# Feed-forward's last two slots begun in the next block, the differential token transposes behind the mask, and products of constants at two passages

## Time and profile before

| | |
|---|---|
| median of 3 runs | 1691.2 us (1690.83 to 1692.31) |
| the profiled execution | 1685.52 us |
| its span, first to last instruction | 1683.8 us |
| its mean granted TensorE clock | 0.984 of full |
| TensorE busy | 95% of the span |
| VectorE, ScalarE, GpSimd busy | 70%, 54%, 40% |
| block 1 ends, block 2 begins | about 395 us |
| block 2 ends, block 3 begins | about 1052 us |
| experts begin | 1599 us |

### The profile page before, as it was taken

The page is one execution under the profiler, slowest core; times in us unless marked ns, Lnnn a source line. Parts: engine busy times, 40 slices in busy tenths (PEclk is TensorE's granted clock), DMA queues, the critical chain, the costliest instruction groups (busy, mean ns, idle before and its releaser), DMA issues. The chain is left out here.

```text
span 1683.8 us, 51948 instructions
## 1 busy us (share of the span) xinstructions
PE 1605.1 (95%) x18158; PEld 1337.3 (79%) x18158; DVE 1183.5 (70%) x3386; ACT 909.4 (54%) x2619; POOL 677.9 (40%) x1070
## 2 busy tenths in 40 slices
PE   7999999998999999999999998899999999999595
PEld 6887788786777777777777776799999999999564
DVE  6889888676777776676777766366777777777654
ACT  5777777543454444454455444555555556565241
POOL 3666655312233333333333332234444444444345
PEclk9999999999999999999999999899999999999898
DMA  3214212121220001110000001121212212122231
GB/s 103 65 47 122 71 55 58 44 57 45 50 53 26 25 26 29 29 28 25 25 25 25 25 27 27 37 58 45 61 46 56 59 42 61 45 56 57 83 95 42
DMA packets 157655, 82.30 MB, mean 49 GB/s; under 512 B 17642, under 2 KB 153116, under 8 KB 157569
## 3 DMA queue, kind: packets, MB, share of 16 engines
q1 hardware_dynamic: 154800, 77.68, 17.3%
q0 software_dynamic: 2048, 3.15, 0.6%
q10 hardware_dynamic: 720, 0.33, 0.1%
HBM read 61.03 MB, written 21.27 MB: 49 GB/s over the span
## 5 line engine op out<-in xcount | busy, mean ns | idle before, releaser
L1445 PE MATMUL bank<-diff_xT,diff_w_score 128*128 128x128 f32 x2048 | 258.9, 280 | 0.8 <-ACT diff_xT L1557 0.8
L1445 PEld LDWEIGHTS bank<-diff_xT,diff_w_score 128*128 128x128 f32 x2048 | 241.5, 193 | 22.4 <-issue 20.2
L1564 ACT ACTIVATE diff_keys<-bank 128x512 f32<-128x512 f32 x256 | 152.4, 595 | 165.3 <-PE bank L1445 165.3
L1754 POOL TENSOR_TENSOR diff_prob<-diff_prob,diff_inv_sum 128x512 f32<-128x512 f32 x64 | 67.2, 1050 | 379.9 <-DVE diff_inv_sum L1657 379.9
L2233 POOL TENSOR_TENSOR lat_prob<-lat_prob,lat_inv_sum 128x512 f32<-128x512 f32 x128 | 133.6, 1044 | 211.0 <-DVE lat_inv_sum L2158 210.0
L2033 ACT ACTIVATE lat_prob<-bank,lat_neg_max 128x128 f32<-128x128 f32 x512 | 180.5, 372 | 1.0 <-DVE lat_neg_max L2178 1.0
L2044 ACT ACTIVATE lat_query<-bank 128x512 f32<-128x512 f32 x128 | 76.4, 597 | 176.6 <-PE bank L1928 176.6
L1958 PE MATMUL bank<-lat_catT,lat_query 128*128 128x128 f32 x1024 | 143.3, 283 | 3.9 <-ACT lat_query L2044 3.9
L1928 PE MATMUL bank<-lat_catT,lat_w_score 128*128 128x128 f32 x1024 | 140.5, 281 | 2.5 <-ACT lat_catT L2025 1.0
L1958 PEld LDWEIGHTS bank<-lat_catT,lat_query 128*128 128x128 f32 x1024 | 126.0, 194 | 16.0 <-issue 10.6
L1938 PE MATMUL bank<-lat_probT,lat_c_rep 32*128 32x256 f32 x2048 | 128.3, 387 | 3.1 <-DVE lat_z L2163 3.1
(11 more groups left out here) (272 smaller groups left out, 3663.6 us busy)
## 6 DMA issues: line engine op xcount, KB each, us to landing
lat_c_rep<-cat SPq DMA_DIRECT2D x128, 128.0 KB
stage<-low_y SPq DMA_DIRECT2D x64, 64.0 KB, 1.6
diff_x_rep<-stage SPq DMA_DIRECT2D x128, 32.0 KB, 1.8
lat_c_t<-cat SPq DMA_DIRECT2D x32, 128.0 KB, 2.2
exp_w<-in_L_ffn_w_dram SPq DMA_DIRECT2D x16, 256.0 KB, 3.1
expert_rows<-latw_zeros SPq DMA_DIRECT2D x4, 548.0 KB, 5.5
exp_rows<-expert_rows SPq DMA_DIRECT2D x8, 274.0 KB, 3.8
low_x_t<-in_x_dram SPq DMA_DIRECT2D x32, 64.0 KB, 1.9
```

The costliest lines, as they stand in the source:

```text
L1445: last = nc.tensor.matmul(ring[(k + d) % 2][:, j * P:(j + 1) * P], w_score[:, H1 * (k // 2) + HS * d + 4 * (k % 2) + j, :], xT[:, :], star ...
L1564: nc.scalar.activation(keys[:, k // 2, 4 * (k % 2):4 * (k % 2) + 4, :].rearrange("p h t -> p (h t)"), ring[(k + d) % 2][:, :], ACT.Copy).t ...
```

## The change

Three edits.

1. The feed-forward's slots 16 and 17 leave block 1 and become the first work of block 2 on TensorE, VectorE, GpSimd and SyncE (`drain`). The feed-forward's tiles, its weights `w_out` and its semaphores are kept over the passage for that. SyncE's wait for the stored groups comes behind its work for pair 0.
2. In block 2 the transpose of the next pair's tokens comes behind the scores and their mask instead of in front of them.
3. `keep_busy` makes products of the bf16 identity with itself repeated (128 x 512, a constant) into a PSUM bank that nobody reads: eight at the end of block 2, 22 between the latent attention and the experts.

```diff
+    def keep_busy(self, bank, count):
+        wide = self.identb[:, None, :].to_broadcast([P, 4, P])
+        for _ in range(count):
+            self.nc.tensor.matmul(bank[:, :].rearrange("p (n d) -> p n d", n=4), self.identb[:, :], wide, start=True, stop=True)
...
@@ FeedForward @@
-        for g in range(NG - 4, NG + 2):
+        for g in range(NG - 4, NG):
             written(g)
+
+    def drain(self, eng, slot):
+        for g in range(self.NG, self.NG + 2):
+            slot(g, g // 4, g % 4, lambda d: 0 <= g + d < self.NG)
...
-    def tensor(self, pe, between=None):
+    def tensor(self, pe, between=None, drain=False):
...
-        pe.wait_ge(self.low.qT_ready, NI)
-        self.slots(pe, slot, between)
+        if drain:
+            self.drain(pe, slot)
+        else:
+            pe.wait_ge(self.low.qT_ready, NI)
+            self.slots(pe, slot, between)
...
@@ differential_attention_phase, sync @@
-            for par in range(2):
-                sp.wait_ge(ffn_stored[par], 16 * (FeedForward.NG // 2))
-            pairs(sp, pair, lambda i: latent.sync(sp, i))
+            def feed_forward_stored(i):
+                if i == 0:
+                    for par in range(2):
+                        sp.wait_ge(ffn.stored[par], 16 * (ffn.NG // 2))
+
+            ffn.sync(sp, drain=True)
+            pairs(sp, pair, lambda i: (feed_forward_stored(i), latent.sync(sp, i)))
...
@@ differential_attention_phase, tensor @@
-                    if d == 1 and more(i):
-                        transpose_x(i + 1)
                     if have(i):
                         if d == 0:
                             pe.wait_ge(tri_done, 4)
                         scores(n)
+                    if d == 1 and more(i):
+                        transpose_x(i + 1)
                     if d == 1 and have(i, 1):
...
+            ffn.tensor(pe, drain=True)
             pe.wait_ge(early.loaded[2], early.all)
             pe.wait_ge(early.wo_loaded, 16)
+            pe.wait_ge(ffn.xT_ready, ffn.NG)
             transpose_x(0)
             pairs(pe, pair)
             latent.products(pe)
+
+            pe.wait_ge(latent.score_copied, 4)
+            core.keep_busy(core.bank[6], 8)
...
@@ differential_attention_phase, vector and gpsimd @@
+            ffn.vector(dve, drain=True)
             for q in range(4):
                 at, s = slice(L * q, L * (q + 1)), L * (q % 2)
                 nc.vector.tensor_copy(tri[at, :], core.causal[at, s:s + L]).then_inc(tri_done, 1)
...
+            ffn.gpsimd(pool, drain=True)
             pool.wait_ge(gb_loaded, 64)
             pairs(pool, pair, lambda i: latent.gpsimd(pool, i))
...
@@ latent_attention_and_experts, tensor @@
             pairs(pe, pair)
+            core.keep_busy(ps_c[3], 22)
             experts.tensor(pe)
```

More of the change, by code:

```diff
@@ L633, with __init__ @@
 class FeedForwardWeights:
-    def __init__(self, core, ctx, loads):
+    def __init__(self, core, ctx, kept, loads):
         self.core, self.nc = core, core.nc
@@ L832, in slot @@
                              self.y[:, m % 2, :, :]).then_inc(self.stored[m % 2], 16)
-        self.slots(sp, slot, between)
-    def tensor(self, pe, between=None):
+        if drain:
+            self.drain(sp, slot)
+        else:
+            self.slots(sp, slot, between)
+    def tensor(self, pe, between=None, drain=False):
         core, nc, GP, NT = self.core, self.nc, self.GP, FF // P
@@ L887, in slot, with vector @@
                         .then_inc(self.relu_done, 1)
-        self.slots(act, slot, between)
-    def vector(self, dve, between=None):
+        if drain:
+            self.drain(act, slot)
+        else:
+            self.slots(act, slot, between)
+    def vector(self, dve, between=None, drain=False):
         nc, GP, NT = self.nc, self.GP, FF // P
@@ L930, in slot, with gpsimd @@
                     .then_inc(self.veps_done, 1)
-        self.slots(dve, slot, between)
-    def gpsimd(self, pool, between=None):
+        if drain:
+            self.drain(dve, slot)
+        else:
+            self.slots(dve, slot, between)
+    def gpsimd(self, pool, between=None, drain=False):
         core, nc = self.core, self.nc
@@ L942, in slot @@
                                         core.eps_pow[:, :].to_broadcast([P, self.GP]), ALU.pow).then_inc(self.rstd_done, 1)
-        self.slots(pool, slot, between)
+        if drain:
+            self.drain(pool, slot)
+        else:
+            self.slots(pool, slot, between)
 def first_layer(core, kept, x_in, kv_in, x_mid, x_out, x_end, loads, early, diff_inputs, lam):
@@ L988, in _ @@
             ffn.gpsimd(pool, lambda g: second.gpsimd(pool, g))
[L990 removed]
+    return ffn
 class EarlyWeights:
```

27 lines of the change are left out of this document (14 added, 13 removed).

## The result

The changed kernel takes **1679.3 us** (median of 5 runs, 1676.6 to 1684.3), the kernel before beside it 1692.3 (5 runs, 1690.8 to 1696.8). The ratio is 0.9916 with a 95% interval of 0.9896 to 0.9935: 0.84% faster, 14 us (11 to 18); the two medians lie 13.0 apart. The forecast was 1680.2. The profiled execution took 1676.6 us, its span is 1674.9 us, its mean granted clock 0.989 instead of 0.984.

What follows compares the result with a forecast made beforehand. It took TensorE, busy 95% of the span, as the bound, with low-clock stretches at three passages. Gains of 4.6 + 2.0 + 2.1 + 2.3 = 11.0 us off the 1691.2 median gave 1680.2 us, range 1675.0 to 1687.0.

Steps and rivals of the forecast that it cites:

- Term 1: Differential attention's loop: the token transpose moved behind the mask saves 0.15 us per pair, 31 pairs, 4.6 us gained.
- The third rival: The loop gains nothing, the transpose's bubble of 0.26 us moving along; passages as forecast: 1684.8 us, chance 0.09.
- the slower one: Loop: gap of 0.20 us before the moved transpose and 0.26 behind, 6.2 lost, passages give nothing: 1697 us, chance 0.06.
- Term 2: First passage, between blocks 1 and 2: output products moved behind the barrier, key products start earlier; 2.0 us gained.
- the middle case: First passage: clock falls in the new idle stretch, output products run low, then dense work lifts it; 2.0 us gained.
- Term 3: Second passage, eight products: 4.4 us gained if the clock stays full, 0.3 lost if it falls; half-way, 2.1 gained.
- the prediction's own sign of being wrong: Wrong if the pair's step is 20.0 or more, transposes have idle time in front, or those groups run at half rate.
- Term 4: Ahead of the experts: 22 products take 7.2 us, end 1.2 before the rows land, and raise the clock; 2.3 us gained.
- full clock at both passages: Clock stays full at the first two passages too: 15.1 us gained, 1676.1 us, chance 0.17.
- clock held nowhere: The products don't hold the clock, or it falls again around the experts' transposes: 4.6 us gained, 1686.6 us, chance 0.18.

Runs made afterwards that it cites:

- the transposes' run: Changed kernel with each product of constants replaced by two fp32 transposes of the 128 x 128 identity: median 1674.7 us, ratio 0.9916.
- the changed kernel's second series: The changed kernel measured once more, unaltered, beside three variants: median 1676.1 us against 1687.3 for the kernel before, ratio 0.9922.
- all pauses filled: Changed kernel plus products of constants in every TensorE pause where a clock of 0.50 was seen: median 1675.8 us, ratio 0.9903.

## Why the prediction was right, and where it wasn't

The number came out 0.9 us from the median, and part of that is luck. The gain by the medians is 13.0 us where 11.0 was forecast. But the forecast started from a median of 1691.2 for the kernel before, and beside the changed kernel it was 1692.3. The two errors partly cancel. The steps, by all profiles that bear on each (seven or more with the edit against three or four without):

| term | forecast | measured |
|---|---|---|
| 1, transpose behind the mask | 4.6 gained | 5.7 gained (620.3 to 620.6 against 626.0) |
| 2, first passage | 2.0 gained | 1.8 in the profile; P1 10.8 to 13.3 in seven profiles, mean 12.4, against 14.9: 2.5 |
| 3, second passage | 2.1 gained, of it 0.3 lost at the barrier | 2.4 in the profile; P2 508.0 to 512.3 in seven, mean 510.3, against 512.9: 2.6, less 0.1 at the barrier |
| 4, ahead of the experts | 2.3 gained | 2.4 in the profile; P3 10.3 in all with the products against 13.0: 2.8 |
| sum | 11.0 | 13.5; by the medians 13.0 |

**Term 1** was right in its mechanism and a little small. The gap ahead of the scores is 0.32 instead of 0.58 and the transpose takes 0.11 behind the mask, both as costed: 0.15. The step fell by 0.19. The other 0.04 lies behind the output products: the first 16 key products took 1.99 and the next work started 1.92 behind their start in the kernel before; now that is 1.95 and 1.88. Timeline of TensorE in the kernel before at that place, behind the earlier trace rows:

```profile
551.51 1.99 PE L1445 MATMUL bank<-diff_xT,diff_w_score 128*128 128x128 f32 x16
553.43 1.14 PE L1457 MATMUL bank<-diff_probT,diff_x_rep 32*128 32x512 f32 x8
```

What the key products paused for there wasn't tried. The third rival (the loop gains nothing) and the slower one (bubble in front and behind) are both out: no idle time stands at the transpose.

**Term 2** went the way of the middle case: the clock was low during the output products and rose during the keys. The barrier cost 1.24 (390.41 to 391.65), not 1.5; the output products took 3.75 and the keys 4.47 instead of 3.91, so the clock came back a little later than forecast. This is the middle case in four of seven profiles (P1 13.06 to 13.31). In two the clock didn't fall at all (10.77), and in one P1 was 12.15. One premise of terms 2 and 3 was one profile's luck: that idleness of 3.0 us leaves the clock up (the stretch from 1573.10). At or just behind that same wait, 3.1 us long, the clock fell in six of the ten profiles in which it wasn't filled. Moving VectorE's norms and SyncE's stores (at 397.05) behind the barrier cost nothing on TensorE's row.

**Term 3** had the right size for a wrong reason. The prediction knew two outcomes, a clock that stays (4.4) or falls (0.3 lost), and took half-way. The profile shows a third: it fell all the same, at 1045.8, and came back at 1052.6 instead of after 13.7 us. Its reason for the low end, that a fall costs what it cost before, was the step that failed, and by the prediction's own sign of being wrong: the first key group still took 2.05 us, not 1.16. Over seven profiles the outcome lies anywhere between: 5.0 gained to 0.7. The second semaphore clear cost 0.13, not 0.3: the barrier stretch is 3.83 or 3.84 in every profile with edit 1 and 3.70 or 3.71 in every one without. The sentence from the Trainium skill, which would have put 0.3 lost here, isn't borne out by the transposes' run.

**Term 4** was right: 6.92 us long against 7.2, 1.53 ahead of the rows against 1.2, hidden products 3.70. The mean of 2.8 is above its upper end of 2.4, since P3 in the profile it was worked out from, 12.71, was the lowest of the four without the products (up to 13.28).

**What the sum left out.** The prediction speaks of three stretches at the low clock. It overlooked a fourth, 3.4 us from 314.8 on in block 1 (and one at the very end), and block 1 is where much of the spread between profiles comes from. And the sum had nothing for the experts' stretch behind term 4, where the changed kernel's first profile lost 3.2 us that no edit had caused. This is why two profiles differ by 8.9 us and the medians by 13: the profile of the kernel before has no late semaphores, that of the changed kernel has. If the kernel before loses as much on such a chip, as its times suggest, the loss drops out between medians taken side by side.

Of the rivals, full clock at both passages (1676.1) came in no profile in which these passages had the changed kernel's products alone, though one of the two was free of low clock three times (the first twice, the second once), and clock held nowhere (1686.6) is excluded by P2 and P3.

## What to carry to other kernels

In this kernel a pause of TensorE could cost twice: the pause, and the products behind it at half rate. Constant products placed in pauses that something else bounded (a barrier, a DMA, another engine's last work) were free as long as they ended before what TensorE waited for. Where the clock was low they took up to twice as long (eleven took 4.20 us, nine at the full clock 2.12), and then they were in the way. When executions of one kernel differ by more than the effect, cut the timeline at fixed instructions and compare stretch by stretch, over several profiles: the median of 12 runs could not see an edit that one stretch showed at once. With most of the low stretches filled, nine executions were enough to see it.

## What the hardware showed that I had not expected

- The clock falls without a long pause. In block 1 it fell at 305 us where TensorE's pauses were 0.45 to 0.74 us long, between small products, and stayed at 0.50 while TensorE was busy for 15.24 of 16.90 us. With nine products of constants in the pauses (about 2 us of work) it didn't fall there in any of four profiles; in two of them it was low for 3.4 us from 313.3 or 314.3 on.
- The same instructions with the same pause may keep the clock or lose it: P1 10.77 and 13.31 us, P2 507.95 and 512.26 us, block 1's end 387.7 and 393.5 us in profiles of kernels that don't differ there. In the changed kernel's second series 1680.6 and 1680.7 us go with a mean clock of 0.984, and 1670.8 and 1672.0 with 0.991: nearly all of its spread of 10 us. With all pauses filled the spread was 2 to 4 us, in fewer executions.
- fp32 transposes alone raised the clock from 0.50 to 1.00 and held it (7.67 us of them ahead of the experts).
- On two chips, and in the changed kernel's first profile, the semaphores of the experts' output products came up to 1.5 us behind their rows, from the second expert on. In the changed kernel's first profile that cost 3.2 us. Its cause is open. The kernel before takes 2 to 4 us more at equal clock on those two chips than on the two others (an estimate), so it probably loses as much.
